# Repeated maxima products in the leads of self and cross attention

## The chip, the cores and the metric

One core of one Trainium2 chip. The metric is the device time of one execution in microseconds, the median of several runs; the kernel before has 874.06 us (three runs, 873.12 to 874.97).

## The reference

Two transformer blocks in sequence on x of 2 x 512 tokens with 320 features, and a context of 2 x 1024 tokens with 192 features. Cut to what matters:

```
# block 0, 8 heads of 40
out = mha(x @ Wq, enc @ Wk, enc @ Wv)                # enc: the context without its last 4 tokens
out = out + mha(mha(ca_q1, x, x) @ Wq, ca @ Wk_ca, ca @ Wv_ca)   # ca: the last 4 tokens
x = out @ Wout + b_out + x
# block 1, 20 heads of 16
x = attn(ln(x), ln(x), q1, k1, v1, o1) + x            # self, 512 keys
x = attn(ln(x), context, q2, k2, v2, o2) + x          # cross, 1024 keys
a, g = split(ln(x) @ ff_w1 + ff_b1)
return a * gelu(g) @ ff_w2 + ff_b2 + x
```

Each attention is softmax(q k^T * scale) v with the maximum of each row taken off.

## The kernel before

An attention runs as a stream: `S_FIRST` (block 0), `S_SELF` and `S_CROSS`. Its heads are packed in groups; a self or cross group has four heads, of 32 rows each. There are 10 groups in self with 4 key tiles each (40 steps) and 10 in cross with 8 (80 steps).

Each score is computed twice. First TensorE forms q k^T with the queries on the partitions, and VectorE reduces it to the row maxima (the maxima pass, in items of 128 queries by 512 keys, from 48 rows of `q_sl` and `k_sl`). The maxima are split, transposed on TensorE (`flip`, L929) and stored as two more rows of `q_sl`. Then TensorE forms the scores again, transposed and with the maxima taken off (50 rows, `scores`, L955), ScalarE takes the exponential (L1057), and TensorE multiplies with the values (`values`, L975).

The maxima pass runs ahead of the scores by a number of chunks, the lead: 8 in self and 12 in cross, of four items each. `pe_attention` issues the lead first and the steps then; everything is written out in the order in which TensorE executes it, and the engines meet in semaphores alone.

- In the self lead projections of q, k and v (`self_side`) are mixed in, two items behind each projection. Its last two chunks (x = 6 and 7) have none left: `share(x)` is empty there. An item (`item`, L918) waits until one of the three banks 4, 5 and 6 is free (`bank_free`), and VectorE reduces each item by itself (L1097).
- In the cross lead (`wide_items`, L895) four products fill the banks 0 to 3 or 4 to 7 in turn, and VectorE reduces all four in one instruction (L1111). A chunk waits until the one before the last is reduced (`score_free`). The products of a chunk lie alternately in rows 0 to 47 and 64 to 111.
- Behind the lead TensorE waits for the side work's evacuation (self) or for the chunk before the last (cross), issues the scores of step 0, and then in each step scores, four maxima items and the values. ScalarE needs the first scores, and TensorE goes on with step 1 when the first exponential has left its banks (`st.exp`).

The lead of `S_FIRST` goes through the same `maxima`, each chunk behind its share of projections.

Of the kernel before, what the change touches and what calls it, by code (L numbers as in the profile page):

```python
# [11 lines left out]
B, SQ, D = 2, 512, 320  # L12
# [16 lines left out]
SBANKS = (4, 5, 6)  # L29
W0, W1 = D0 + 2, D1 + 1  # L30
V0, V1 = H0 * W0 + 64 - W0, H1 * W1 + 32 - W1
OBANK = 7


class Attention:
# [112 lines left out]
def build(nc, ins, out_dram):  # L148
# [117 lines left out]
    PS = nc.alloc_psum_tensor("PS", [128, 8, 512], F32)  # L266
# [271 lines left out]
    first = Projection("first", first_jobs())  # L538
    second = Projection("second", second_jobs(), (0, 1, 2), (3, OBANK), first)
    selfp = Projection("selfp", self_jobs(), (2, 3, OBANK))  # L540
# [144 lines left out]
    for st in (S_FIRST, S_SELF, S_CROSS):  # L685
        n = st.name
# [39 lines left out]
    def q_view(g):  # L726
        a = g.a
        return g.q_t[:, 0:a.inner * a.nq].rearrange("p (i n) -> p i n", i=a.inner)

    def k_view(g):  # L730
        a = g.a
        return g.k_t[:, 0:a.inner * a.row].rearrange("p (i n) -> p i n", i=a.inner)
# [134 lines left out]
    def wide_bank(c):  # L867

        return 4 * (c % 2)
# [8 lines left out]
    def pe_attention(pe, st, side=None):  # L878
        wide = st is S_CROSS

        def wide_items(c):
            per = st.groups[0].a.per_step
            if c >= 2:
                pe.wait_ge(st.score_free, per * (c - 1))
            for n, (i, m) in enumerate(st.chunk(c)[1]):
                g = st.groups[i]
                a = g.a
                j, q, part = a.items[m]
                if m == 0:
                    pe.wait_ge(q_loaded[g.place], g.loads)  # L890
                if n == 3 and c and st.chunk(c - 1)[0] is not None:
                    pe.wait_ge(st.flipped, st.chunk(c - 1)[0] + 1)
                c0, cn = a.chunks[part]
                f = a.base(j)
                nc.tensor.matmul(PS[0:a.qt, wide_bank(c) + n, 0:cn],  # L895
                                 q_view(g)[f:f + a.rows, j // a.stack, q * a.qt:(q + 1) * a.qt],
                                 k_view(g)[f:f + a.rows, j // a.stack, c0:c0 + cn],
                                 start=True, stop=True).then_inc(st.score, 1)
            if st.chunk(c)[0] is not None:
                pe.wait_ge(st.score_free, per * c)  # L900
                flip(st.chunk(c)[0], waits=False)

        def bank_free(k):
            if k >= 3:
                by, n = st.freed_by[k - 3]
                pe.wait_ge(st.score_free if by == "item" else st.flipped, n)

        def item(i, m):
            g = st.groups[i]
            a = g.a  # L910
            j, q, c = a.items[m]
            k = st.item_use[i, m]
            if m == 0:
                pe.wait_ge(q_loaded[g.place], g.loads)
            bank_free(k)
            c0, cn = a.chunks[c]
            f = a.base(j)
            nc.tensor.matmul(PS[0:a.qt, SBANKS[k % 3], 0:cn],  # L918
                             q_view(g)[f:f + a.rows, j // a.stack, q * a.qt:(q + 1) * a.qt],
                             k_view(g)[f:f + a.rows, j // a.stack, c0:c0 + cn],  # L920
                             start=True, stop=True).then_inc(st.score, 1)

        def flip(i, waits=True):
            g = st.groups[i]
            a = g.a
            pe.wait_ge(st.m_low, i + 1)
            if waits:
                bank_free(st.flip_use[i])
            nc.tensor.transpose(PS[0:2 * a.cols, flip_bank(st, i), 0:a.qt],  # L929
                                mparts[0:a.qt, g.turn, 0:2 * a.cols].bitcast(F32),  # L930
                                ident[0:a.qt, 0:a.qt]).then_inc(st.flip, 1)

        def maxima(chunks, first=0, last=None):

            for c in chunks:
                for i, m in st.chunk(c)[1][first:last]:
                    item(i, m)

        def flips(chunks):
            for c in chunks:  # L940
                if st.chunk(c)[0] is not None:
                    flip(st.chunk(c)[0])

        def scores(i, t, p):
            g = st.groups[i]
            a = g.a
            sz = a.size[t]
            if t == 0 and p == 0:
                pe.wait_ge(g.m_sem, g.m_loads)
            x = st.first_pair[i] + t * a.pairs + p  # L950
            pe.wait_ge(st.exp, x + 1)
            for half in range(2):
                j = 2 * p + half
                f = a.base(j)
                mm = nc.tensor.matmul(PS[0:sz, 2 * (x % 2) + half, 0:a.nq],  # L955
                                      k_view(g)[f:f + a.rows + 2, j // a.stack, t * 128:t * 128 + sz],
                                      q_view(g)[f:f + a.rows + 2, j // a.stack, :], start=True, stop=True)
            mm.then_inc(st.pair, 1)

        def values(i, t, p):  # L960
            g = st.groups[i]
            a = g.a
            sz, w = a.size[t], a.width
            if t == 0 and p == 0:
                pe.wait_ge(st.out_read, i + 1)
                if a is A_CA and g.n == 0:
                    pe.wait_ge(x_filled, TT)
            x = st.first_pair[i] + t * a.pairs + p
            pe.wait_ge(st.exp, x + 3)
            per = a.groups // B  # L970
            tile = g.n // per * (a.row // 128) + t
            for half in range(2):
                j = 2 * p + half
                h = g.n % per * a.g + j
                mm = nc.tensor.matmul(PS[w * j:w * j + w, OBANK, 0:a.nq],  # L975
                                      a.vc[0:sz, tile, a.vw * h:a.vw * h + w],
                                      probs[0:sz, x % PRING, half, 0:a.nq],
                                      start=(t == 0), stop=(t == a.kt - 1), tile_position=(0, w * j))
            mm.then_inc(st.used, 1)

        for x in range(st.lead):
            if wide:
                wide_items(x)
            elif side is self_side:
                among = 2 if x else 0
                for n, (ph, j) in enumerate(side.share(x)):
                    pe_projection(pe, ph, [j])
                    maxima([x], among * n, among * (n + 1))
                maxima([x], among * len(side.share(x)))
                flips([x])  # L990
            else:
                for ph, j in side.share(x):
                    pe_projection(pe, ph, [j])
                maxima([x])
                flips([x])
        if wide:
            pe.wait_ge(st.score_free, st.groups[0].a.per_step * (st.lead - 1 + st.lead % 2))
        for ph in side.phases if side is not None else []:
            if ph.ns:
                pe.wait_ge(ph.low, ph.ns)  # L1000
            if ph.nv:
                pe.wait_ge(ph.padded, ph.nv)
        one = st.groups[0].a.pairs == 1
        for s in range(2 if one else 1):
            for p in range(st.groups[0].a.pairs):
                scores(*st.steps[s], p)
        if one:
            for s in range(0, len(st.steps), 2):
                for u in (s, s + 1):
                    if u + 2 < len(st.steps):  # L1010
                        scores(*st.steps[u + 2], 0)
                    maxima(st.chunks_at(u))
                values(*st.steps[s], 0)
                values(*st.steps[s + 1], 0)
                if s >= len(st.steps) - 8:
                    pe_ca_keys(pe, (s - len(st.steps) + 8) // 2)
                for u in (s, s + 1):
                    flips(st.chunks_at(u))
        else:
            for s in range(len(st.steps)):  # L1020
                if s + 1 < len(st.steps):
                    scores(*st.steps[s + 1], 0)
                maxima(st.chunks_at(s), 0, 2)
                if s + 1 < len(st.steps):
                    scores(*st.steps[s + 1], 1)
                maxima(st.chunks_at(s), 2, 3)
                for p in range(2):
                    values(*st.steps[s], p)
                maxima(st.chunks_at(s), 3)
                flips(st.chunks_at(s))  # L1030
# [858 lines left out]
```

## Time and profile before

| | us |
|---|---|
| median of three runs | 874.06 |
| span of the profiled execution, first to last instruction | 871.2 |
| TensorE busy | 809.5 (93%) |
| VectorE busy | 596.4 (68%) |
| ScalarE busy | 474.1 (54%) |
| mean granted clock of TensorE | 0.963 |

The profile is of one execution. Its own time is known by the span alone; the median of the runs is 2.9 us over it, for what lies before the first and behind the last instruction. PE is TensorE's products, PEld its weight loads, DVE VectorE, ACT ScalarE, POOL GpSimd. A granted clock of 1.00 is 2.4 GHz and 0.50 is 1.2 GHz. A product's busy time includes its way through the array, so that products that follow each other overlap. A product of f32 operands that are not rounded (values) has two records.

### The profile page before, as it was taken

What the parts mean: (1) busy time and instruction counts of PE and PEld (TensorE: products, weight loads), DVE (VectorE), ACT (ScalarE), POOL (GpSimd) and SP (SyncE); (2) the same over time, 40 slices, a digit from 0 to 9 for tenths busy, and PEclk for the clock granted to TensorE, in tenths of its full rate; (3) what the DMA queues carried; (4) which work ended last, traced back from release to release, by engine and by line L of the source; (5) the groups of instructions that cost most, each with busy time, mean ns of one, the idle gap of its engine ahead of it and who ended that gap; (6) DMA issues with size and microseconds to landing.
All of it is one profiled execution on the core that took longest, in us unless ns stands there. A gap on an engine that the chain in (4) does not pass through costs nothing.

```text
span 871.2 us, 11443 instructions
## 1 busy us (share of the span) xinstructions
PE 809.5 (93%) x4148; PEld 443.6 (51%) x4148; DVE 596.4 (68%) x1068; ACT 474.1 (54%) x720; POOL 119.5 (14%) x197
## 2 busy tenths in 40 slices
PE   5999999999999998999989659999999999899998
PEld 3777644444466665333326323333333333678888
DVE  4455576777675557799947587999999971784231
ACT  4643454445544533576687225777667778863130
POOL 4100104100005332000014400000000000540000
PEclk9999999999999998799999857999999999999999
DMA  8886578523310174122134500222232000600000
GB/s 294 269 283 199 153 224 271 132 70 88 100 40 32 68 253 112 39 75 74 39 73 74 194 1 20 48 52 51 56 56 56 2 2 1 257 0 1 31 1 31
DMA packets 30966, 83.18 MB, mean 95 GB/s; under 512 B 5172, under 2 KB 9212, under 8 KB 28606
## 3 DMA queue, kind: packets, MB, share of 16 engines
q1 hardware_dynamic: 30110, 79.71, 31.9%
q0 software_dynamic: 800, 2.73, 0.9%
q8 instruction: 33, 0.54, 0.3%
q14 instruction: 23, 0.19, 0.1%
HBM read 56.12 MB, written 25.89 MB: 94 GB/s over the span
## 4 chain that ended last, share of the span: by engine, by line
PE 65%; DVE 15%; DMA 9%; ACT 5%; issue 4%; SPq 2%; POOL 0%; ACTq 0%; DVEq 0%; POOLq 0%
PE PS L975 19%; PE PS L918 14%; PE PS L1570 8%; PE PS L955 7%; PE PS L619 6%; DVE maxp L1097 5%; DMA k_d<-split 4%; PE PS L1588 4%; DVE negm L1097 3%; PE PS L1389 2%; DMA q_sl<-msplit 2%; ACT probs L1057 2%; DVE maxp L1111 2%; DVE turned L1143 1%; DMA w_raw<-in_ff_w 1%
## 5 line engine op out<-in xcount | busy, mean ns | idle before, releaser
L1057 ACT ACTIVATE probs<-PS 128x1024 f32<-128x1024 f32 (+1 forms) x336 | 310.4, 971 | 139.9 <-PE PS L955 137.0
L1097 DVE TENSOR_REDUCE maxp<-PS 128x1 f32<-128x512 f32 (+1 forms) x400 | 251.6, 678 | 43.4 <-PE PS L918 42.4
L918 PE MATMUL PS<-k_sl,q_sl 48*128 48x512 f32 (+2 forms) x592 | 225.5, 455 | 10.0 <-DVE maxp L1097 2.0
L955 PE MATMUL PS<-q_sl,k_sl 50*128 50x512 f32 (+3 forms) x672 | 203.9, 435 | 9.9 <-ACT probs L1057 6.0
L918 PEld LDWEIGHTS PS<-k_sl,q_sl 48*128 48x128 f32 (+2 forms) x592 | 103.5, 190 | 168.0 <-DVE maxp L1097 105.8
L1097 DVE TENSOR_REDUCE negm<-PS 128x1 f32<-128x512 f32 (+1 forms) x192 | 121.5, 677 | 27.7 <-PE PS L918 27.1
L955 PEld LDWEIGHTS PS<-q_sl,k_sl 50*128 50x128 f32 (+2 forms) x672 | 102.8, 192 | 56.8 <-ACT probs L1057 25.4
L975 PE MATMUL PS<-probs,v2c 128*32 128x512 f32 x640 | 88.1, 620 | 1.0
L661 DVE TENSOR_TENSOR split<-PS,split 128x512 fp32r<-128x512 f32 (+3 forms) x54 | 34.9, 649 | 54.8 <-ACT split L636 54.6
L975 PE MATMUL PS<-probs,v0c 128*64 128x512 f32 (+1 forms) x256 | 62.0, 605 | 0.0
L636 ACT CAST split<-PS 128x512 fp32r<-128x512 f32 (+3 forms) x54 | 29.9, 554 | 53.5 <-PE PS L619 38.8
L1143 DVE STREAM_TRANSPOSE turned<-PS 128x512 f32<-128x512 f32 (+1 forms) x36 | 22.9, 636 | 43.8 <-PE PS L975 43.3
L1570 PE MATMUL PS<-act_high,w_high 128*128 128x512 f32 x120 | 47.5, 395 | 3.3 <-DVE w_low L1546 2.0
L975 PE MATMUL PS<-probs,v1c 128*32 128x512 f32 x320 | 45.5, 639 | 2.1 <-DVE turned L1143 1.2
L1570 PE MATMUL PS<-act_high,w_low 128*128 128x512 f32 x120 | 46.8, 390 | 0.0
L1040 ACT CAST msplit<-PS 32x128 fp32r<-32x128 f32 (+2 forms) x36 | 8.9, 249 | 54.6 <-PE PS L929 54.6
L1202 POOL TENSOR_TENSOR packed<-turned,recip 128x256 f32<-128x256 f32 x20 | 12.7, 633 | 174.0 <-DVE recip L1146 174.0
L1462 ACT ACTIVATE act_t<-PS,params 128x128 f32<-128x128 f32 x72 | 27.7, 455 | 12.7 <-PE PS L1407 12.7
L1570 PE MATMUL PS<-act_low,w_high 128*128 128x512 f32 x80 | 31.2, 390 | 0.0
L1631 DVE SCALAR_TENSOR_TENSOR ff_raw<-PS,params,gelu 128x512 f32<-128x512 f32 x20 | 15.0, 748 | 22.5 <-ACT gelu L1611 22.5
L1541 ACT CAST ff_high<-ff_raw 128x512 fp32r<-128x512 f32 x20 | 12.4, 622 | 32.8 <-DVE ff_raw L1631 32.8
L1189 POOL CAST mparts<-negm 128x16 fp32r<-128x16 f32 x20 | 3.9, 196 | 188.8 <-DVE negm L1078 101.7
(186 smaller groups left out, 1072.6 us busy)
## 6 DMA issues: line engine op xcount, KB each, us to landing
k_d<-split SPq DMA_DIRECT2D x20, 512.0 KB, 3.9
q_d<-split SPq DMA_DIRECT2D x12, 512.0 KB, 4.0
k_sl<-k_d SPq DMA_DIRECT2D x8, 640.0 KB
k_sl<-k_d SPq DMA_DIRECT2D x40, 128.0 KB
q_sl<-q_d SPq DMA_DIRECT2D x40, 128.0 KB
k_sl<-k_d SPq DMA_DIRECT2D x20, 256.0 KB
w_raw<-in_ff_w SPq DMA_DIRECT2D x1, 3840.0 KB, 11.6
k_sl<-k_d SPq DMA_DIRECT2D x8, 320.0 KB
```

The costliest lines, as they stand in the source:

```text
L619: mm = nc.tensor.matmul(o, w, a, start=(k == 0), stop=(k == len(j["mm"]) - 1))
L636: nc.scalar.copy(split[0:j["m"], ph.slot(i), 0, 0:j["n"]], split_bank(ph, j)).then_inc(ph.high, 1)
L661: nc.vector.tensor_tensor(split[0:j["m"], ph.slot(i), 1, 0:j["n"]], split_bank(ph, j), split[0:j["m"], ph.slot(i), 0, 0:j["n"]].bitcast(F3 ...
L918: nc.tensor.matmul(PS[0:a.qt, SBANKS[k % 3], 0:cn], q_view(g)[f:f + a.rows, j // a.stack, q * a.qt:(q + 1) * a.qt], k_view(g)[f:f + a.rows ...
L955: mm = nc.tensor.matmul(PS[0:sz, 2 * (x % 2) + half, 0:a.nq], k_view(g)[f:f + a.rows + 2, j // a.stack, t * 128:t * 128 + sz], q_view(g)[f ...
L975: mm = nc.tensor.matmul(PS[w * j:w * j + w, OBANK, 0:a.nq], a.vc[0:sz, tile, a.vw * h:a.vw * h + w], probs[0:sz, x % PRING, half, 0:a.nq], ...
L1057: nc.scalar.activation(probs[0:a.size[t], x % PRING, :, 0:a.nq], PS[0:a.size[t], 2 * (x % 2):2 * (x % 2) + 2, 0:a.nq], ACT.Exp, scale=a.sc ...
L1097: nc.vector.tensor_reduce((maxp if nch > 1 else negm)[0:a.qt, g.turn, o:o + 1], PS[0:a.qt, SBANKS[k % 3], 0:a.chunks[c][1]], AX.X, ALU.max ...
L1143: nc.vector.transpose(turned[:, 0:a.nq], PS[:, OBANK, 0:a.nq]).then_inc(st.out_read, 1)
L1462: o = nc.scalar.activation(act_t[0:fn, m, t * 128:(t + 1) * 128], PS[0:fn, 4 + t % 2, 128 * m:128 * m + 128], ACT.Identity, bias=params[0: ...
L1570: mm = nc.tensor.matmul(PS[:, up_bank(i, part), :], w[:, k, f0:f0 + 128], a[:, k, cols], start=(n == 0), stop=(n == len(UP_TERMS) - 1))
L1588: mm = nc.tensor.matmul(PS[:, 4 + t % 4, 0:D], a[:, m, rows], w[:, m, :], start=(m == 0 and n == 0), stop=(m == FT - 1 and n == 2))
```

## The change

The same products are issued several times. `REPEATS` is a new constant.

- `wide_items` (cross lead): before the first product of each chunk, the same product four times, into the same bank.
- `item` takes `repeats`; `maxima` passes it on. In the self lead the items that follow no projection any more (the last two chunks) have each product two times more, into its own bank, behind the bank wait.
- Behind the lead of self and of cross, eight products of group 0's queries and keys into bank 2, ahead of the first scores. (`one` is true for `S_FIRST` alone, which has none.)

A repeat has no semaphore; its result is overwritten by the product that follows in that bank.

```diff
+REPEATS = 4
@@ wide_items
+                for _ in range(REPEATS if n == 0 else 0):
+                    nc.tensor.matmul(PS[0:a.qt, wide_bank(c) + n, 0:cn],
+                                     q_view(g)[f:f + a.rows, j // a.stack, q * a.qt:(q + 1) * a.qt],
+                                     k_view(g)[f:f + a.rows, j // a.stack, c0:c0 + cn],
+                                     start=True, stop=True)
@@ item
-        def item(i, m):
+        def item(i, m, repeats=0):
...
+            for _ in range(repeats):
+                nc.tensor.matmul(PS[0:a.qt, SBANKS[k % 3], 0:cn],
+                                 q_view(g)[f:f + a.rows, j // a.stack, q * a.qt:(q + 1) * a.qt],
+                                 k_view(g)[f:f + a.rows, j // a.stack, c0:c0 + cn], start=True, stop=True)
@@ maxima
-        def maxima(chunks, first=0, last=None):
+        def maxima(chunks, first=0, last=None, repeats=0):
...
-                    item(i, m)
+                    item(i, m, repeats)
@@ the lead
-                maxima([x], among * len(side.share(x)))
+                maxima([x], among * len(side.share(x)), repeats=0 if side.share(x) else 2)
@@ behind the lead
         one = st.groups[0].a.pairs == 1
+        for _ in range(0 if one else REPEATS * 2):
+            g = st.groups[0]
+            nc.tensor.matmul(PS[:, 2, 0:SQ], q_view(g)[0:g.a.rows, 0, 0:128], k_view(g)[0:g.a.rows, 0, 0:SQ],
+                             start=True, stop=True)
```

## Rows read from the trace of the kernel before

**Rows 1.** The page: the span in 40 equal slices, 21.8 us each.
```profile
PE   5999999999999998999989659999999999899998
...
PEclk9999999999999998799999857999999999999999
```

**Rows 2.** Busy time by windows: PE, PEld, DVE, ACT, POOL, clock, DMA share, GB/s.
```profile
500.00:505.00 5.00, 2.53 (x10) 1.01 (x8) 5.00 (x3) 0.00 (x0) 0.00 (x0) 0.50 0.00 0
...
525.00:530.00 5.00, 5.00 (x22) 2.15 (x20) 3.31 (x6) 2.28 (x3) 0.00 (x0) 0.50 0.00 0
```

**Rows 3.** Busy time by windows, narrow ones, where the granted clock changes.
```profile
340.90:341.00 0.10, 0.10 (x1) 0.00 (x0) 0.10 (x2) 0.00 (x0) 0.10 (x1) 0.50 0.00 0
...
361.00:362.00 1.00, 1.00 (x8) 0.41 (x9) 1.00 (x3) 1.00 (x2) 0.00 (x0) 0.81 0.44 131
...
494.00:495.00 1.00, 0.53 (x2) 0.50 (x4) 1.00 (x2) 0.00 (x0) 0.00 (x0) 0.75 1.08 320
...
532.00:533.00 1.00, 1.00 (x10) 0.62 (x7) 0.17 (x1) 0.00 (x0) 0.00 (x0) 0.98 0.00 0
```

**Rows 4.** Timeline of PE, behind the self lead: start us, us, what.
```profile
343.13 1.43 PE L955 MATMUL PS<-q_sl,k_sl 50*128 50x512 f32 x4
...
346.61 0.79 PE L955 MATMUL PS<-q_sl,k_sl 50*128 50x512 f32 x2 [2.05 <-ACT probs L1057]
...
361.69 1.06 PE L975 MATMUL PS<-probs,v1c 128*32 128x512 f32 x8
```

**Rows 5.** Timeline of PE before, in and behind the cross lead.
```profile
488.33 0.39 PE L619 MATMUL PS<-x_mixed,w_q_high 128*64 128x512 f32 x1
...
488.55 0.39 PE L619 MATMUL PS<-x_mixed,w_s_low 128*64 128x512 f32 x1
...
491.25 1.20 PE L895 MATMUL PS<-k_sl,q_sl 48*128 48x512 f32 x8 [1.39 <-DVE split L661]
...
494.48 1.22 PE L895 MATMUL PS<-k_sl,q_sl 48*128 48x512 f32 x4 [2.03 <-DVE maxp L1111]
...
511.10 2.40 PE L895 MATMUL PS<-k_sl,q_sl 48*128 48x512 f32 x8
...
517.00 1.22 PE L955 MATMUL PS<-q_sl,k_sl 50*128 50x512 f32 x4 [0.97 <-DVE maxp L1111]
...
520.26 0.80 PE L955 MATMUL PS<-q_sl,k_sl 50*128 50x512 f32 x2 [2.03 <-ACT probs L1057]
...
520.85 0.63 PE L918 MATMUL PS<-k_sl,q_sl 48*128 48x512 f32 x2
...
521.27 0.69 PE L955 MATMUL PS<-q_sl,k_sl 50*128 50x512 f32 x2
...
522.32 1.93 PE L975 MATMUL PS<-probs,v2c 128*32 128x512 f32 x8
...
526.48 1.93 PE L975 MATMUL PS<-probs,v2c 128*32 128x512 f32 x8
...
534.00 1.06 PE L975 MATMUL PS<-probs,v2c 128*32 128x512 f32 x8
```

**Rows 6.** Timeline of DVE in both leads.
```profile
338.59 6.07 DVE L1097 TENSOR_REDUCE negm<-PS 128x1 f32<-128x512 f32 x10 [0.57 <-PE PS L918]
...
492.13 17.68 DVE L1111 TENSOR_REDUCE maxp<-PS 128x4 f32<-128x2048 f32 x8 [0.93 <-PE PS L895]
...
512.46 6.69 DVE L1111 TENSOR_REDUCE maxp<-PS 128x4 f32<-128x2048 f32 x3 [0.24 <-PE PS L895]
```

**Rows 7.** Timeline of ACT behind both leads.
```profile
344.24 1.28 ACT L1057 ACT_TABLE_LOAD   x1 [5.65 <-PE PS L955]
...
517.89 1.28 ACT L1057 ACT_TABLE_LOAD   x1 [6.42 <-PE PS L955]
```

**Rows 8.** Busy time by windows: slow head and rest of each stream.
```profile
361.69:440.00 78.31, 75.90 (x448) 27.90 (x447) 74.18 (x128) 55.46 (x63) 7.35 (x21) 1.00 0.19 57
...
534.00:740.00 206.00, 199.92 (x1194) 73.02 (x1194) 173.83 (x296) 150.09 (x162) 10.08 (x28) 1.00 0.19 36
```

## The prediction

> **What bounds the kernel now.** I read the slices of the page first, then the busy time by windows, then the timelines of TensorE, VectorE and ScalarE around the two places that the slices pointed to. In the slices TensorE is busy nearly everywhere, and the granted clock is at its upper level (2.4 GHz) except in two dips, which fall on the leads of the self and the cross stream [rows 1]. The narrow windows date them. The clock falls to 1.2 GHz at 340.9 us and is back at 361.3; it falls again at about 494.5 us and is back at 532.0 [rows 3]. So 20.4 + 37.5 = 58 us run at half clock.
>
> What does that cost? Inside the cross lead, nothing. There VectorE reduces one chunk of four banks after the other with hardly a break: eight reductions in 17.68 us, or 2.20 us each, while TensorE is busy 2.53 us of five [rows 2, 6]. The four products of a chunk take 1.22 us at half clock [rows 5] and wait for a bank. The self lead is the same on a smaller scale: ten reductions in 6.07 us, 0.60 us each [rows 6].
>
> The cost begins behind the leads. From the moment that TensorE goes on with scores, values and later maxima, it is busy without a break at half clock (5.00 of 5.00 us) and VectorE only 3.31 of 5 [rows 2]. A step takes 4.16 us there (values of the cross stream at 522.32 and 526.48) [rows 5]. At full clock VectorE is the engine that has no slack, with 173.83 of 206.00 us, and a step has 16 product records, so 206.00 us with 1194 records are 74.6 steps of 2.76 us. The self stream has 78.31 us with 448 records, 28 steps of 2.80 us [rows 8]. The slow head of self runs from 346.61 to the fourth group of values at 361.69, 15.08 us; that of cross from 520.26 to 534.00, 13.74 us [rows 4, 5, 8]. At full clock each would be a start of some 1.4 us (2.06 us from 520.26 to 522.32 at half clock; half of it is 1.03 and no shortening 2.06, and I take a value between) and three steps: 1.4 + 3 x 2.80 = 9.8 and 1.4 + 3 x 2.76 = 9.7. So **at most 5.3 + 4.0 = 9.3 us** are to be won, and only if the clock is at its upper level behind the leads.
>
> **The change part by part.** It removes nothing and adds no wait, no DMA and no work on other engines. It adds TensorE products with their weight loads: in the self lead 2 before each of the 8 items of its last two chunks (16), in the cross lead 4 before the first product of each of 12 chunks (48), and 8 behind each lead (16). In all 80. Each stands behind the bank wait of the product that it repeats, so it delays that product, and whatever stands behind it in TensorE's queue.
>
> Price of one repeat. No row shows a repeat. The nearest at full clock are projections of the same 512 columns, one behind the other in the same rows: they start at 488.33 and 488.55, 0.22 us apart, and a few at 0.23 or 0.24 [rows 5]. I take 0.23. The cross products lie in pairs in different rows, eight in 1.20 us with the last one's own 0.4 in it, so 0.27 a pair or 0.13 a product [rows 5]; if repeats overlapped like that, 0.13. At half clock starts are 0.42 apart (520.85 to 521.27), and a pair in the lead takes 2.40 / 4 = 0.60 at most [rows 5].
>
> Repeats in the self lead. An item is now three products. Neighbouring items lie in different rows, and in cross such products run side by side [rows 5], so an item adds about 2 x 0.23 = 0.46 us to TensorE's stream against the 0.60 us of VectorE's reduction [rows 6], and three banks let it run ahead. Cost 0 while the clock is high; the last item comes 2 x 0.23 = 0.46 us later. Without the overlap it is 0.69 against 0.60, 0.5 us in all.
>
> Repeats in the cross lead. In a running chunk 4 x 0.23 + about 0.5 = 1.4 us fit into 2.20, so they are hidden under VectorE. They are not hidden in two places. VectorE has nothing to do before the first chunk is complete, so the four repeats there cost 4 x 0.23 = 0.9 us. After the flip of group 0, for which TensorE has to wait, the products start at 511.10, and VectorE already waits 0.24 us for them and starts at 512.46 [rows 5, 6]. That is 1.36 us from the first start to VectorE. With four repeats at full clock it is 4 x 0.23 = 0.92 for them, about 0.3 for the first pair and 0.55 for the second with the hand-over, 1.8 in all, and VectorE starts 0.4 us later. Cross lead: 1.3 us (0.6 with overlapped repeats, 2.4 + 1.0 = 3.4 if these eight ran at 0.60).
>
> Eight behind each lead. They stand in front of the first scores, and the first scores are what ScalarE waits for: at 517.89 it starts its table load (1.28 us) and then the first exponential, and TensorE goes on at 520.26 when that is done [rows 5, 7]. Nothing hides them. VectorE has no work left until TensorE goes on, and the cover that it gave in the lead is gone. Cost 8 x 0.23 = 1.8 us each. In cross the scores then take 0.3 us less at full clock (517.00 to 517.89 is 0.9; 0.6 in its place), net 1.5. In self the same gain stands against the 0.46 of the last item, less some 0.2 that TensorE runs ahead: 1.7 us [rows 4, 7]. Bounds for each group of eight: 1.0 and 4.8.
>
> Sum of the costs: 1.7 + 1.3 + 1.5 = **4.5 us** (bounds 2 and 13).
>
> What comes back? In the leads the clock should hold. It fell at 340.9 with single products 0.60 apart and at 494.5 behind an idle gap of 2.03 us between the second and third chunk [rows 3 to 6]. With the repeats TensorE is busy nearly through in self and about 1.4 of 2.2 us in cross, and the 2.03 us gap shrinks to about 1.2. But behind the eight and the scores comes a gap that no repeat fills: table load, exponential and hand-over, 2.37 us from ScalarE's start until TensorE goes on [rows 5, 7]. Less the scores still running it is 2.1 to 2.4 us, as long as the one behind which the clock fell at 494.5 or longer. Unless it comes at a lucky moment the clock falls in it or just behind it. Then the streams start at half clock as now, and the trace shows how long that lasts: TensorE fully busy from 346.61 and yet slow until 361.3, from 520.26 until 532.0 [rows 3 to 5]. The fall comes perhaps 0.5 us behind the restart, which gives 0.2 to 0.3 us back in each stream.
>
> The row shows a fall behind a gap of 2.03 us [rows 3, 5]. The Trainium skill (TensorE: Matmul & The Clock Gate, "Why this matters for your kernels") only warns of gaps over some 3 us between bursts of products; by that the new gap of 2.4 us would be harmless and the sum -4.8 us instead of +4.0. The measured fall at 494.5 speaks against it.
>
> **Forecast.** 4.5 - 0.5 = +4.0 us. The profiled span is 871.2 us, so 875.2. The median of the runs is 874.06, 2.9 us over the span, which the change doesn't touch: **878.1 us**. With the lead's bounds its own range is 876 to 881.
>
> **The rivals.**
> (1) The clock holds through both gaps. For it: the lead just before is dense now, while before 494.5 there were only eight products in over three microseconds [rows 5]; against it: the length of the gap. Price: +4.5 - 9.3 = -4.8, so 869.3 us. It decides at the first values behind the leads: if they come 2.8 us apart, it is this.
> (2) It holds in one stream and falls in the other, depending on where the gap falls by chance. Self held: 4.5 - 5.3 - 0.3 = -1.1; cross held: 4.5 - 4.0 - 0.3 = +0.2. About 873.6 us.
> (3) The repeats don't hold the clock even in the leads. For it: they fill 48 of 128 rows, the engine still pauses for a bank in each chunk of cross, and with such products alone the trace shows no stretch at full clock. At half clock a chunk takes 1.22 + 4 x 0.42 = 2.9 us against VectorE's 2.20, so 0.7 us of each of some nine chunks show (6), plus first chunk and flip (2), the eight (8 x 0.42 = 3.4, twice), and in self 6 x 0.26 = 1.6: +16, so 890 us; with the clock back in part of the lead, since TensorE would be full there, about half of it: 882. The point from which it decides is a chunk period over 2.3 us.
> The Trainium skill has a rule for (3), in TensorE: Matmul & The Clock Gate, "A second HAM failure mode: psum-queue depth-cycling": short pauses between groups of products, while PSUM banks are cycled, are enough to make the clock swing. The trace agrees for the present lead (low from 494.5 on), and no run here shows it for a denser one.
>
> **How the numbers follow.** Forecast 0.40, (1) 0.23, (2) 0.22, (3) 0.15. Under 0.2% (1.75 us) either way can't be told from no change. Faster: 0.23 of (1) and 0.05 of (2), where self alone holds and the cheaper repeats apply: 0.28. Same: the rest of (2) and a little of the forecast's lower end, 0.20. Slower: 0.52. The range leaves out (3) at full price and the better half of (1): 868.5 to 884.
>
> **What would show it.** Right: granted clock 1.00 in the cross lead with VectorE's reductions still 2.20 us apart; ScalarE's table loads about 1.7 (self) and 2.8 us (cross) later relative to the start of each lead; a TensorE gap of over 2 us behind the scores, a fall to 0.50 there, and three values groups about 4.2 us apart. Wrong: values 2.8 us apart from the first on (rival 1), or clock 0.50 and TensorE full inside the cross lead (rival 3). My weakest step is how often the clock falls in the gap.

## The result, and the profile after

The kernel with the change takes 885.17 us (median of four runs, 882.28 to 888.76) against 873.59 us before (868.5 to 874.97): a ratio of **1.0149, 95% interval 1.0111 to 1.0186**. It is slower, by some 12 to 13 us, and outside the range of the prediction (868.5 to 884). The profiled execution has a span of 884.3 us, 13.1 us more than the span before. Its own time is 886.18, 1.9 us over its span, and so it is, within 0.2 us, in every run here; of the 2.9 us that stood between span and median before, some 1 us was the difference between one execution and the median.

The page of the changed kernel, its slices of 22.1 us (the answer to [rows 1]):

```profile
PE   5999999999999999999989898999999999899998
...
PEclk9988999999999997699999757999999999999999
```

TensorE is busier in the leads than before, and the clock is no better: the dips on the two leads are still there, and longer. Busy time by windows (columns as in [rows 2]): start of the cross lead, the rest of it, the eight products and the scores, the slow head of the steps:

```profile
495.63:498.00 2.37, 2.37 (x14) 1.95 (x15) 0.57 (x1) 0.00 (x0) 0.00 (x0) 0.99 1.04 365
...
498.00:527.96 29.96, 28.73 (x85) 18.99 (x83) 24.74 (x12) 0.26 (x1) 0.42 (x2) 0.50 0.11 33
...
527.96:532.09 4.13, 4.13 (x13) 2.95 (x12) 2.29 (x1) 0.00 (x0) 0.00 (x0) 0.50 0.00 0
...
534.46:542.30 7.84, 7.84 (x31) 2.84 (x31) 4.37 (x7) 4.74 (x5) 0.00 (x0) 0.50 0.00 0
```

From 498.0 us on the clock is at 1.2 GHz, and TensorE is busy 28.73 of the 29.96 us of the cross lead. Before it was busy half of the time there, at the same clock [rows 2]. So being busy with these products did not keep the clock up. In self it falls at 341 and is back at 368.3 (before: 340.9 and 361.3, [rows 3]).

VectorE in both leads (timeline, the answer to [rows 6]; the idle time before a row stands in brackets):

```profile
337.89 4.48 DVE L1111 TENSOR_REDUCE negm<-PS 128x1 f32<-128x512 f32 x7 [0.57 <-PE PS L928]
...
342.71 2.09 DVE L1111 TENSOR_REDUCE negm<-PS 128x1 f32<-128x512 f32 x3 [0.34 <-PE PS L928]
...
497.43 4.49 DVE L1125 TENSOR_REDUCE maxp<-PS 128x4 f32<-128x2048 f32 x2 [1.86 <-PE PS L901]
...
502.84 2.29 DVE L1125 TENSOR_REDUCE maxp<-PS 128x4 f32<-128x2048 f32 x1 [0.93 <-PE PS L901]
...
505.40 2.29 DVE L1125 TENSOR_REDUCE maxp<-PS 128x4 f32<-128x2048 f32 x1 [0.27 <-PE PS L901]
...
508.26 2.29 DVE L1125 TENSOR_REDUCE maxp<-PS 128x4 f32<-128x2048 f32 x1 [0.56 <-PE PS L901]
...
522.89 2.29 DVE L1125 TENSOR_REDUCE maxp<-PS 128x4 f32<-128x2048 f32 x1 [1.52 <-PE PS L901]
...
528.30 2.29 DVE L1125 TENSOR_REDUCE maxp<-PS 128x4 f32<-128x2048 f32 x1 [0.56 <-PE PS L901]
```

This is the place to read. A wide reduction started every 2.20 us before; now two take 5.42 us (502.84 to 508.26), 2.71 each, and each has idle time before it (0.27 or 0.56 us in a running lead, 0.93 where the clock has just fallen, 1.52 behind the flip) that a product ended. TensorE has become the bound of the lead. ScalarE's table loads (the answer to [rows 7]) and TensorE behind the lead (the answer to [rows 5]):

```profile
347.22 1.28 ACT L1071 ACT_TABLE_LOAD   x1 [9.33 <-PE PS L965]
...
532.09 1.28 ACT L1071 ACT_TABLE_LOAD   x1 [11.91 <-PE PS L965]
```

```profile
527.96 2.76 PE L1016 MATMUL PS<-k_sl,q_sl 48*128 48x512 f32 x6
...
534.46 0.79 PE L965 MATMUL PS<-q_sl,k_sl 50*128 50x512 f32 x2 [2.03 <-ACT probs L1071]
...
536.53 1.93 PE L985 MATMUL PS<-probs,v2c 128*32 128x512 f32 x8
...
546.89 1.07 PE L985 MATMUL PS<-probs,v2c 128*32 128x512 f32 x8
```

Where the 13.1 us went, by the two profiled executions, in us:

| stretch | before | after | more |
|---|---|---|---|
| self: ten reductions, from the first start to the last end | 6.07 | 6.91 | 0.8 |
| self: from there to the table load | -0.42 | 2.42 | 2.8 |
| cross: first product to first reduction | 0.88 | 1.80 | 0.9 |
| cross: first to last reduction start | 24.74 | 30.87 | 6.1 |
| cross: last reduction start to table load | 1.02 | 3.79 | 2.8 |
| cross: table load to the fourth values | 16.11 | 14.80 | -1.3 |

That is 12.1. The self head (the steps behind the lead, until the clock is back) is 1.4 longer (table load to the fifth values: 364.59 - 344.24 = 20.35 before, 368.95 - 347.22 = 21.73 after), and the kernel came to the self lead 0.7 us earlier: 12.8, with 0.3 left in the rest. How long a head stays at half clock differs from one execution to the next. The self stream of `cross_lead_only` (below) is that of the kernel before, and its profile shows the dip from 340.0 to 353.7, 13.7 us in place of 20.4. So the two head terms (1.4 and -1.3) can be chance. The other five stand where the added products stand; the first of them, 0.8, also depends on when the clock falls.

### The profile page after: what moved, and what is told of

Read it like the earlier page. It is cut to its first block, busy times and chain, and to the rows that moved or that the text cites. A ratio compares the mean times of both kernels' runs of the same rounds, so it can differ in the third digit from the quotient of the medians.

```text
span 884.3 us, 11603 instructions
## 1 busy us (share of the span) xinstructions
PE 836.4 (95%) x4228; PEld 466.9 (53%) x4228; DVE 597.3 (68%) x1068; ACT 474.5 (54%) x720; POOL 120.2 (14%) x197
## 4 chain that ended last, share of the span: by engine, by line
PE 73%; DVE 13%; DMA 5%; ACT 4%; issue 3%; SPq 1%; POOL 0%; ACTq 0%; DVEq 0%; POOLq 0%
PE PS L985 18%; PE PS L928 14%; PE PS L620 11%; PE PS L1584 8%; PE PS L965 7%; DVE maxp L1111 5%; PE PS L1602 4%; PE PS L1403 2%; DVE negm L1111 2%; DMA q_sl<-msplit 2%; ACT probs L1071 2%; PE PS L897 2%; DVE turned L1157 1%; DMA w_raw<-in_ff_w 1%; DMA k_d<-split 1%
## 5 line engine op out<-in xcount | busy, mean ns | idle before, releaser
L1125 DVE TENSOR_REDUCE maxp<-PS 128x4 f32<-128x2048 f32 x12 | 27.4, 2291 | 7.4 <-PE PS L901 7.4
## 6 DMA issues: line engine op xcount, KB each, us to landing
k_d<-split SPq DMA_DIRECT2D x20, 512.0 KB, 4.0
q_d<-split SPq DMA_DIRECT2D x12, 512.0 KB, 3.9
```

## The experiments

Three theories. **A, the rows**: products that fill 48 of the array's 128 rows don't keep the clock up or bring it back; products of 128 rows do. **B, the pauses**: the engine's pauses for a bank bring the clock down, whatever the products are. **C, the queue alone**: the repeats cost their own time in front of what others wait for, and the clock has no part in it. Each kernel ran 12 times, on the same chip as 35 runs of the kernel before. There were three such groups, on three chips, with medians before of 872.55, 871.73 and 871.50 us, so kernels of different groups are compared by their ratios. In the ratios 1 us is 0.00115. A profile shows one of the 12 executions; where it matters the mean granted clock of all 12 is given beside it.

### One part of the change at a time

```diff
 # cross_lead_only: wide_items as changed; maxima(..., repeats=0); no products behind the leads
 # self_lead_only: item with 2 repeats in the last two chunks; nothing else
 # eights_only: the eight products behind each lead; nothing else
```

> Of the change only the four repeats before each chunk of the cross lead (48 rows). From the two traces the cross lead has a chunk in 2.71 us instead of 2.20 while the clock is low. All theories: the lead is some 6 us longer than before (table load of cross at +6), 879 to 881. Under theory A the clock is at 0.50 from the second or third chunk on, although TensorE hardly pauses.

Measured: 878.04 us, ratio 1.0072 (1.0043 to 1.0101), 6.3 us, against the expected 6. The cross lead has the pattern of the changed kernel. The window over it, at a mean clock of 0.52:

```profile
489.00:520.70 31.70, 30.22 (x95) 19.95 (x93) 25.73 (x13) 0.30 (x2) 0.42 (x2) 0.52 0.17 51
```

and three of its wide reductions, 2.85 and 2.56 us apart:

```profile
497.38 2.29 DVE L1121 TENSOR_REDUCE maxp<-PS 128x4 f32<-128x2048 f32 x1 [0.27 <-PE PS L901]
...
500.23 2.29 DVE L1121 TENSOR_REDUCE maxp<-PS 128x4 f32<-128x2048 f32 x1 [0.56 <-PE PS L901]
...
502.79 2.29 DVE L1121 TENSOR_REDUCE maxp<-PS 128x4 f32<-128x2048 f32 x1 [0.27 <-PE PS L901]
```

> Of the change only the eight products behind each lead. At half clock 8 x 0.43 = 3.4 us in front of each first score, twice: +6.8 us if nothing comes back, 881. If the clock were raised by them (against theory A), the slow heads would be shorter and it would be under 876.

Measured: 878.54 us, ratio 1.0057 (1.0031 to 1.0083), 5.0 us; the expected 6.8 lies inside the interval (2.7 to 7.2). The self group (timeline of PE): six of the eight take 2.90 us at half clock, and the gap behind the scores is what it was.

```profile
344.55 2.90 PE L1011 MATMUL PS<-k_sl,q_sl 48*128 48x512 f32 x6
...
351.21 0.80 PE L960 MATMUL PS<-q_sl,k_sl 50*128 50x512 f32 x2 [2.06 <-ACT probs L1066]
```

> Of the change only the two repeats of each item in the last two chunks of the self lead. Theory A: the clock falls at about the same place as before (near 341), an item then takes 2 x 0.43 = 0.86 us against 0.60 of the reduction: +1 to +2 us, 875. Theory B (pauses): with hardly a pause left the clock holds in the self lead and the table load comes no later.

Measured: 871.87 us, ratio 1.0000 (0.9974 to 1.0025). No cost and no gain can be told; the interval is 2.2 us to either side, so the +1 to +2 of theory A isn't excluded. In its profile the clock did hold through the lead until 345.7, and was back at 359.4; so in this part theory B is not excluded by the one trace. Over the 12 executions nothing came of it: their mean granted clocks are 0.957 to 0.970, those of the kernel before 0.955 to 0.970.

6.3 + 5.0 + 0.0 = 11.3 us: the parts add up to the change (ratio 1.0149, 13 us) within their intervals.

### The same repeats with 128 rows

```diff
-nc.tensor.matmul(PS[...], q_view(g)[f:f + a.rows, ...], k_view(g)[f:f + a.rows, ...], start=True, stop=True)
+nc.tensor.matmul(PS[...], x_high2[:, 0, 0:128], x_high2[:, 1, 0:512], start=True, stop=True)   # at all three places
```

`x_high2` is the rounded input of the projections, 128 rows of it; the results are overwritten as before.

> The 80 repeats stay where they are, but each is a product of 128 rows by 128 columns (x_high2, as stationary and as moving operand) in place of 48 by 128; the time of one is the same. Theory A (products that fill 48 of the 128 rows don't keep the clock up or raise it): the clock stays at 1.00 through both leads, chunks of the cross lead are 2.20 us apart again in place of 2.71, and the time falls to 868 to 879, depending on whether the clock falls in the gap behind the scores. Theory B (the pauses for a bank bring the clock down, whatever the rows): clock 0.50 in the cross lead as now, 885. Theory C (the repeats cost their time in the queue, and the clock has no part in it): 885.

Measured: 879.29 us, ratio 1.0087 (1.0053 to 1.0121). In the profiled execution the clock did what A said; the median time didn't, and lies at the upper end of A's range. The window over the cross lead, VectorE's first eight reductions in it, and TensorE from the gap on:

```profile
491.00:520.40 29.40, 24.32 (x109) 13.04 (x107) 26.75 (x13) 0.26 (x1) 0.42 (x2) 1.00 0.19 57
```

```profile
492.59 17.68 DVE L1120 TENSOR_REDUCE maxp<-PS 128x4 f32<-128x2048 f32 x8 [2.06 <-PE PS L899]
```

```profile
522.80 0.50 PE L962 MATMUL PS<-q_sl,k_sl 50*128 50x512 f32 x2 [2.22 <-ACT probs L1066]
...
524.41 1.93 PE L982 MATMUL PS<-probs,v2c 128*32 128x512 f32 x8
...
528.28 1.07 PE L982 MATMUL PS<-probs,v2c 128*32 128x512 f32 x8
```

Clock 1.00 throughout the cross lead, with TensorE *less* busy (24.32 of 29.40 us) than at half clock; eight reductions in 17.68 us, as before the change. TensorE still pauses for a bank in each chunk, which speaks against B. The clock falls behind the gap of 2.22 us, at the first values (1.93 us for eight records, at half clock), and is back by the second (1.07). Behind the same gap in self, in the same trace, it doesn't fall:

```profile
351.10 0.50 PE L962 MATMUL PS<-q_sl,k_sl 50*128 50x512 f32 x2 [2.25 <-ACT probs L1066]
...
352.66 1.06 PE L982 MATMUL PS<-probs,v1c 128*32 128x512 f32 x8
```

The next values start at 355.62, 3.0 us later with a flip between them. The time was paid elsewhere. In the self lead, timeline of PE and then of DVE:

```profile
338.46 0.73 PE L923 MATMUL PS<-x_high 128*128 128x512 f32 x2
...
339.12 0.49 PE L925 MATMUL PS<-k_sl,q_sl 48*128 48x512 f32 x1
...
339.54 0.73 PE L923 MATMUL PS<-x_high 128*128 128x512 f32 x2
```

```profile
340.73 0.69 DVE L1106 TENSOR_REDUCE negm<-PS 128x1 f32<-128x512 f32 x1 [0.39 <-PE PS L925]
...
341.82 0.69 DVE L1106 TENSOR_REDUCE negm<-PS 128x1 f32<-128x512 f32 x1 [0.40 <-PE PS L925]
```

In the changed kernel an item and the repeats of its neighbour, in the other row half, start together (339.21 and 339.24). Here they don't: a repeat of 128 rows lies in the way of both row halves. An item takes 1.09 us instead of 0.60, eight of them 3.9 us more. (Three products one behind the other at 0.23 would be 0.69; the starts are 0.3 to 0.4 apart here, and no run tells why.) With 2 x 1.8 for the eights and 1.3 in the cross lead, both as the prediction priced them, some 8.8 us are paid at full clock: an estimate. What comes back for it differs between executions. The profiled one took 873.82 us and is one of the fastest of the 12, which run from 873.69 to 885.39 at mean clocks of 0.938 to 0.994. It lies 1.3 us over the median of before, so it gave most of the 8.8 back, and the median gave little: 7.6 us measured. Where the clock fell in the slower ones no trace shows. Theory C is right about the price of these repeats.

The repeats in the cross lead alone, with 128 columns and with 32:

```diff
-PS[0:a.qt, wide_bank(c) + n, 0:cn], q_view(g)[...], k_view(g)[...]
+PS[0:128, wide_bank(c) + n, 0:cn], x_high2[:, 0, 0:128], x_high2[:, 1, 0:cn]     # cross_full_rows
+PS[0:32, wide_bank(c) + n, 0:cn], x_high2[:, 0, 0:32], x_high2[:, 1, 0:cn]       # cross_full_32cols
```

> Only the four repeats before each chunk of the cross lead, each of 128 rows by 128 columns. Against the same repeats with 48 rows it tells what the rows do. Theory A (rows): clock 1.00 in the cross lead, wide reductions 2.20 us apart, table load of cross some 2 us later than before; the clock falls in the gap behind the scores in most executions, 873 to 876. Theory B (pauses for a bank): clock 0.50 in the lead, 878.

> As before, but the stationary operand of a repeat has 32 columns: 128 rows by 32 columns. If rows alone count, the clock holds as with 128 columns. If it is the filled part of the array (rows times columns, a quarter here, less than the 48 by 128 of the change), the clock falls in the cross lead and stays at 0.50, with wide reductions about 2.7 us apart, 878.

Measured: 875.39 us, ratio 1.0044 (1.0022 to 1.0067), and 875.37 us, ratio 1.0043 (1.0018 to 1.0068). Windows over the cross leads and VectorE's rows, first of the one, then of the other:

```profile
495.00:522.00 27.00, 22.02 (x93) 11.41 (x89) 24.54 (x13) 0.26 (x1) 0.42 (x2) 0.94 0.21 65
```

```profile
495.48 17.68 DVE L1118 TENSOR_REDUCE maxp<-PS 128x4 f32<-128x2048 f32 x8 [2.06 <-PE PS L899]
...
517.53 6.69 DVE L1118 TENSOR_REDUCE maxp<-PS 128x4 f32<-128x2048 f32 x3 [1.95 <-PE PS L899]
```

```profile
491.00:517.70 26.70, 20.78 (x98) 7.87 (x97) 25.16 (x13) 0.26 (x1) 0.42 (x2) 1.00 0.22 70
```

```profile
491.95 17.68 DVE L1118 TENSOR_REDUCE maxp<-PS 128x4 f32<-128x2048 f32 x8 [1.98 <-PE PS L899]
...
512.61 6.69 DVE L1118 TENSOR_REDUCE maxp<-PS 128x4 f32<-128x2048 f32 x3 [0.56 <-PE PS L899]
```

Mean clock 0.94 and 1.00 against 0.52 with 48 rows, and reductions 2.20 us apart. It is not a matter of one profile: over the whole kernel the 12 executions have mean clocks of 0.971 to 0.982 and 0.969 to 0.980, those of `cross_lead_only` 0.951 to 0.967. The columns of the stationary operand made no difference here; a product of 128 by 32 fills less of the array (4096 cells) than one of 48 by 128 (6144). So rows, and not columns or the filled part, set these two kinds apart from the change's. One thing changed together with the rows: the operands are `x_high2` instead of the queries and keys, with other values in them, and no run separates the two. Both still lose 3 to 4 us: the first chunk, the chunk behind the flip (before the last three reductions VectorE is idle 1.95 us in the first, where the clock was low for a moment, and 0.56 in the second), and the clock falls again in the gap behind the scores.

### The gap behind the scores

```diff
 for p in range(st.groups[0].a.pairs):
+    for _ in range(7 if p else 0):
+        nc.tensor.matmul(PS[:, 2, 0:SQ], x_high2[:, 0, 0:128], x_high2[:, 1, 0:SQ], start=True, stop=True)
     scores(*st.steps[s], p)
```

The seven stand, in self and in cross, behind the first pair of scores, which starts ScalarE, and in front of the second, which ScalarE needs only after the table load and the first exponential. Nothing else is changed from the kernel before.

> The kernel before, with no repeats in the leads and none behind them; instead seven products of 128 by 128 stand between the first pair of scores and the second, where TensorE waits for the table load and the first exponential anyway. Theory A: they cost 0 to 1.3 us at half clock (7 x 0.43 = 3.0 against a wait of some 2.5), and raise the clock earlier in the slow heads, by a few us each: 866 to 870. If the gap has no part in it: 872 to 875.

> As the kernel with seven products in the gap behind the first pair of scores, but the products have 48 rows by 128 columns. Theory A (rows): they don't raise the clock, so nothing comes back: the slow heads stay as long as before, and what they cost in the queue (0 to 1.3 us in each stream) is lost: 872 to 875 against a kernel before of about 872. Theory D (the gap need only be filled, with anything): 868, as with 128 rows.

Measured with 128 rows: 868.31 us, ratio **0.9967 (0.9951 to 0.9983)**; with 48 rows 874.17 us, ratio 1.0031 (1.0001 to 1.0061). Same places, same number, and about the same time for each product at half clock. Timelines of PE in self, 128 rows and then 48:

```profile
345.84 3.35 PE L1007 MATMUL PS<-x_high 128*128 128x512 f32 x7
...
351.75 1.06 PE L975 MATMUL PS<-probs,v1c 128*32 128x512 f32 x8
...
354.69 1.06 PE L975 MATMUL PS<-probs,v1c 128*32 128x512 f32 x8
```

```profile
347.06 2.33 PE L1008 MATMUL PS<-k_sl,q_sl 48*128 48x512 f32 x5
...
351.85 0.79 PE L955 MATMUL PS<-q_sl,k_sl 50*128 50x512 f32 x2 [0.33 <-ACT probs L1061]
...
353.00 1.93 PE L975 MATMUL PS<-probs,v1c 128*32 128x512 f32 x8
...
357.92 1.93 PE L975 MATMUL PS<-probs,v1c 128*32 128x512 f32 x8
```

With 128 rows the clock is back before the first values, and these are 2.9 us apart; with 48 they are 4.9 apart (a flip lies between in both), and the clock is low until 365.4. The two profiles are among the slower ones of their kernels, but all 12 executions agree: mean clocks of 0.971 to 0.976 with 128 rows, 0.955 to 0.968 with 48. This is the plainest test of A. Neither B nor C has a reason for it, and D, that the gap need only be filled with anything, is refuted. The values in the operands changed here too.

In cross the same seven did less. They run from 516.16 us in the profile with 128 rows, and the clock is back at 528.2 only: the values start at 522.57, 526.73 and 530.11. That is some 12 us from the first of the seven, against 5 in self. With 48 rows they start at 521.87, and the clock is back at 539.4. So 128 rows bring the clock back earlier in both streams, but not by themselves at once; why it takes longer in cross is open.

> Five products of 128 by 128 in the gap in place of seven: 5 x 0.43 = 2.2 us at half clock, just the length of the wait, so the second exponential is not held up. If the clock rises as with seven, 1 us better than seven (867 to 868); if it rises later or seldom, 870.

Measured: 869.98 us, ratio 0.9981 (0.9962 to 1.0001). Not better than seven; the intervals overlap, so five against seven stays open.

### Both together

```diff
 # lead_and_gap
+for _ in range(4 if n == 0 and c not in (0, 9) else 0):   # wide_items, 128 rows
+for _ in range(repeats if m % 2 == 0 else 0):             # item, one, 128 rows, last two chunks
+    ...                                                   # seven in the gap, none behind the leads
 # lead3_flip_gap, lead2_flip_gap: 3 or 2 in wide_items, none in item, seven in the gap, and before the flip
     pe.wait_ge(st.score_free, per * c)
+    for _ in range(3):
+        nc.tensor.matmul(PS[0:128, wide_bank(c + 1), 0:SQ], x_high2[:, 0, 0:128], x_high2[:, 1, 0:SQ],
+                         start=True, stop=True)
     flip(st.chunk(c)[0], waits=False)
```

> Repeats of 128 by 128 in the cross lead without the chunks 0 and 9 (where VectorE waits), one in front of every second item in the last two self chunks, none behind the leads, and seven in the gap behind the first scores. Theory A: clock 1.00 through both leads and gaps, values 2.8 us apart from the first on, no delay of the leads over 0.5 us each: 9.3 us less than before but for what the clock had there by chance, 863 to 866. Theory C (repeats cost their time in the queue): 872 or more.

Measured: 869.22 us, ratio 0.9967 (0.9945 to 0.9988). Faster than before, but less than expected, and no faster than the seven alone. Theory A's 1.00 through both leads did not come: the clock fell at the pause for the flip in cross (506.7 to 517.0), and in self at 339.5, in the lead with its one product of 128 rows to two items, until 346.3.

> Cross lead with three repeats of 128 by 128 before each chunk but 0 and 9, three more while TensorE waits for the maxima of the flip, seven in both gaps, none in the self lead. If the fall in the flip's pause is what kept the clock down at the end of the cross lead (506.7 to 517.0 in the last trace), it holds at 1.00 from the cross lead to the steps, and the time is 864 to 867.

Measured: 866.39 us, ratio **0.9956 (0.9934 to 0.9978)**, the lowest here. It is below the kernel before and the changed one; from the two kernels with 0.9967 it can't be told, for the intervals overlap. In self, where its lead has no repeats, the clock still fell (341.3 to 348.1). Window over its cross lead, the next 24.5 us, and VectorE at the end of the lead, which now has no pause at the flip:

```profile
488.88:515.50 26.62, 20.09 (x87) 10.12 (x86) 26.59 (x13) 1.74 (x3) 0.42 (x2) 1.00 0.20 59
...
515.50:540.00 24.50, 23.39 (x140) 8.88 (x138) 20.93 (x36) 18.48 (x21) 0.42 (x2) 1.00 0.20 38
```

```profile
506.69 8.88 DVE L1123 TENSOR_REDUCE maxp<-PS 128x4 f32<-128x2048 f32 x4
```

> The same with two repeats before a chunk. Two pairs and two repeats are about 1.0 of 2.2 us busy: the clock is expected to fall in the lead in some executions, 865 to 869. A chunk takes 0.9 + 0.86 us then, still under the 2.20 of the reduction, so no time is lost in the lead itself.

Measured: 870.65 us, ratio 0.9990 (0.9967 to 1.0013). This can't be told from no change. With two repeats in place of three the clock fell in the cross lead (491.5 to 512.0 in the profile) and again at 515.4.

## Why the prediction was wrong

**The step that failed** is "In the leads the clock should hold", and with it the price of a repeat. I argued that a denser TensorE holds the clock. For the leads the trace of before had nothing to show it: its only stretches with such products alone were sparse ones, so sparse and narrow could not be told apart there. Rival (3) named it, "they fill 48 of 128 rows", and what the trace shows is that rival: chunk period 2.71 us, over the 2.3 that I set as its mark. I gave it 0.15. There was a hint in the rows that I read past: behind the leads TensorE was busy 5.00 of 5.00 us [rows 2] and the clock still took until 532.0 to come back [rows 3]. Eight of the 16 product records of such a step have 48 or 50 rows; the other eight, the values, have 128 rows and take 1.93 of its 4.16 us. A busy engine that stays at 1.2 GHz should have moved weight from the forecast to (3).

There was a stronger one that I missed. The prediction says that the clock is at its upper level except in two dips. There is a third, from 61.0 to 67.8 us (the two alone would leave a mean clock of 0.967; it was 0.963); windows of the kernel before, columns as in [rows 2]:

```profile
64.00:66.00 2.00, 2.00 (x7) 1.71 (x7) 0.26 (x1) 0.43 (x1) 0.00 (x0) 0.50 1.04 391
66.00:68.00 2.00, 2.00 (x8) 1.62 (x7) 0.45 (x1) 0.59 (x1) 0.00 (x0) 0.54 0.24 81
```

It begins with a dozen products of 8 columns and two of 4 rows; from 63.06 us on TensorE has nothing but products of 120 and 128 rows, and the clock is back 4.8 us later. Behind the leads, just as full, it took 11.7 us (520.26 to 532.0) and 14.7 us (346.61 to 361.3). These are single dips and not a proof: in `full_rows` the steps behind the cross lead had the clock back within some 3.4 us (524.3 to 527.7). And the dip at 61.0 begins behind a pause of 1.84 us in work of 128 rows, so rows do not keep the clock up through every pause.

- *Repeats in the self lead*, forecast 0 to 0.5: 0.8 in the profile, 0.0 +- 2.2 us alone. Not refuted, but the reason was wrong halfway: in the profile the clock fell within these items.
- *Repeats in the cross lead*, forecast 1.3: 7.0 in the profile, 6.3 alone. The first chunk was right (0.9 for 0.9). The other 6.1 is the half clock: four repeats at 0.43 and the chunk's own products make 2.71 us, no longer hidden under 2.20. So the term was mis-sized through the clock alone. My bound of 3.4 priced the repeats at half clock only where they were in the open and forgot that at half clock they come into the open in every chunk.
- *Eight behind each lead*, forecast 1.7 and 1.5: 2.8 and 2.8 in the profile, 5.0 together alone. That they lie on the path was right, for 2.8 of their 3.4 us; they ran at 0.43 instead of 0.23.
- *What comes back*, forecast 0.5: 1.3 in one head, -1.4 in the other. That the clock would not outlast the gap could not be tested, for it was low already. Where it was high, with 128 rows in `full_rows`, it fell behind the gap of 2.22 us in cross, as the 2.03 us of before had suggested, and held behind the gap of 2.25 us in self. A gap of this length is enough in some cases and not in others, as rival (2) had it.
- Rival (3)'s price of 16 us for a lead at half clock throughout was near the measured 13; the halving to 882, on the ground that a full TensorE would bring the clock back in the lead, was the same error again.

The Trainium skill (TensorE: Matmul & The Clock Gate, "Part 1: The HAM clock gate") says that the gate follows how busy TensorE has been and that activity releases it. The trace disagrees if busy is read as the profile's busy time: in the changed kernel's cross lead that is nearly all of it, at half clock. The warning of the Trainium skill (TensorE: Matmul & The Clock Gate, "Why this matters for your kernels") is of gaps over some 3 us; it would let gaps of 2.22 and 2.25 us pass. The trace of `full_rows` agrees for the second and disagrees for the first, behind which the clock fell.

What stays open: whether it is the rows alone or also the values in the operands, which no kernel changed by themselves; whether it needs all 128 rows or something between 48 and 128, since no kernel tried one; how many products a gap needs, and why the seven worked faster in self than in cross; and in the self lead, why the clock held longer in the one trace with 48 row repeats.

## What to carry to other kernels

Make a filler product (one whose result nobody reads) tall in the contraction: here 48 rows cost as much time as 128, 0.23 us a product at full clock, and did not hold TensorE's clock. Put it where TensorE waits for another engine and nothing behind it is awaited, here between the first scores, which start ScalarE, and the second; in front of an awaited product, or in the way of products that overlap by rows, it costs its full time and more. A busy engine that stays at half clock in the profile before is a sign that more of the same work will bring the clock back late or not at all. And expect little: the best of these kernels gains 0.4%, and one run of each would not have shown it.

## What the runs showed of the hardware

- With repeats of 48 rows TensorE was busy 28.73 of 29.96 us and stayed at 1.2 GHz; with repeats of 128 rows by 128 columns or by 32 columns, from another operand, it stayed at 2.4 GHz through the same lead (busy 24.32 of 29.40 and 20.78 of 26.70 us).
- Seven products of 128 rows in a gap at half clock had it back some 5 us after their start in self (345.84 to 350.7) and some 12 us after in cross (516.16 to 528.2). With seven of 48 rows it was some 18 us in both (347.06 to 365.4, 521.87 to 539.4).
- Behind a TensorE gap of 2.22 us the clock fell, and behind one of 2.25 us in the same execution it didn't (`full_rows`).
- Products in different row halves start together (339.21 and 339.24 in the changed kernel); a product of 128 rows between them ends that: items 1.09 us apart instead of 0.60 at full clock.
- The same program differs by 11 us between runs (867.04 to 878.51 in 35), and the mean granted clock goes with it: 0.970 in the fastest, 0.955 in the slowest.
